# Making the slots' token numbers in two runs of small matmuls in the set-up of a mixture-of-experts kernel

## The reference, cut to what matters

```
gate = xn @ wg_W + wg_b + (genre_embed @ gg_W + gg_b)
gate_w = softmax(gate)
topk_w, topk_i = top_k(gate_w, 2)            # two of eight experts per token
h1 = relu(x @ W1[e] + b1[e]); h2 = relu(h1 @ W2[e] + b2[e])
out_e = h2 @ W3[e] + b3[e]
out = sum over e of out_e * cw[e]            # cw: weight of the chosen experts, else 0
```

## Time and profile before

| | |
|---|---|
| time, median of 3 runs | 742.73 us (741.77 to 743.66) |
| time of the profiled execution | 744.68 us |
| its span, first to last instruction | 743.2 us |
| mean granted TensorE clock over the span | 0.986 of full speed |
| PE busy | 713.3 us, 96% |
| DVE, ACT, POOL busy | 65%, 39%, 12% |

### The profile page before, as it was taken

The page is one execution under the profiler, slowest core; times in us unless marked ns, Lnnn a source line. Parts: engine busy times, 40 slices in busy tenths (PEclk is TensorE's granted clock), DMA queues, the critical chain, the costliest instruction groups (busy, mean ns, idle before and its releaser), DMA issues.

```text
span 743.2 us, 20463 instructions
## 1 busy us (share of the span) xinstructions
PE 713.3 (96%) x8266; PEld 615.5 (83%) x8266; DVE 486.3 (65%) x1036; ACT 287.8 (39%) x839; POOL 90.9 (12%) x102
## 2 busy tenths in 40 slices
PE   6389999999999999999999999999999999999997
PEld 4279999559999999978778878978888897888785
DVE  4756565743545444334777787787778778777867
ACT  3032121142121221253465446445544654564552
POOL 2121112411111101031101101110110111000000
PEclk9599999999999999999999999999999999999999
DMA  7998111217111102310001000000110010000000
GB/s 262 336 353 322 37 37 56 81 43 257 50 37 37 37 30 69 118 50 23 16 9 30 30 7 25 30 23 10 30 31 9 23 30 24 8 16 16 9 9 23
DMA packets 21402, 49.13 MB, mean 66 GB/s; under 512 B 3323, under 2 KB 14971, under 8 KB 18749
## 3 DMA queue, kind: packets, MB, share of 16 engines
q1 hardware_dynamic: 12256, 32.47, 12.2%
q0 software_dynamic: 3744, 10.49, 4.7%
q10 hardware_dynamic: 5309, 4.87, 2.0%
HBM read 41.00 MB, written 6.82 MB: 64 GB/s over the span
## 4 chain that ended last, share of the span: by engine, by line
PE 94%; DVE 3%; ACT 1%; issue 1%; another core or an unknown queue 0%; DVEq 0%; POOL 0%; ACTq 0%; POOLq 0%
PE ps L897 16%; PE ps L796 15%; PE ps L766 8%; PE ps L923 8%; PE ps L830 7%; PE ps L982 7%; PE ps L948 4%; PE ps L998 3%; PE ps L941 2%; PE ps L973 2%; PE ps L1013 2%; PE ps L1075 2%; PE ps L1032 2%; PE ps L790 1%; PE ps L676 1%; PE ps L1045 1%
## 5 line engine op out<-in xcount | busy, mean ns | idle before, releaser
L897 PE MATMUL ps<-arena,l_weights 128*128 128x128 f32 x1024 | 125.9, 277 | 0.5 <-ACT arena L1470 0.5
L796 PE MATMUL ps<-h_t,w_now 128*128 128x128 f32 x1056 | 123.4, 275 | 1.2 <-DVE h_t L1951 1.2
L796 PEld LDWEIGHTS ps<-h_t,w_now 128*128 128x128 f32 x1056 | 120.5, 192 | 1.4 <-issue 1.4
L897 PEld LDWEIGHTS ps<-arena,l_weights 128*128 128x128 f32 x1024 | 119.3, 192 | 2.3 <-ACT arena L1470 1.0
L1395 ACT ACTIVATE h_t<-ps,cols 128x128 f32<-128x128 f32 x132 | 37.8, 367 | 163.9 <-PE ps L766 149.5
L1926 DVE COPY w_now<-arena 128x2048 f32 x33 | 40.5, 1227 | 83.2 <-PE ps L796 74.7
L1476 ACT ACTIVATE arena<-ps,cols 128x128 f32<-128x128 f32 x256 | 73.9, 387 | 48.0 <-PE ps L897 48.0
L645 POOL DMA_INDIRECT arena<-expert_out,slot_of x32 | 33.1, 1033 | 323.0 <-DVE arena L1979 272.8
L766 PEld LDWEIGHTS ps<-xg_t,w_now 128*128 128x128 f32 x528 | 63.4, 192 | 6.0 <-ACT xg_t L1378 3.5
L766 PE MATMUL ps<-xg_t,w_now 128*128 128x128 f32 x528 | 65.0, 276 | 3.0 <-ACT xg_t L1378 3.0
L612 POOL DMA_INDIRECT xg<-in_x,slot_tok x36 | 41.6, 1155 | 186.4 <-PE ps L745 157.4
(11 more groups left out here) (366 smaller groups left out, 1097.1 us busy)
## 6 DMA issues: line engine op xcount, KB each, us to landing
arena<-in_experts SPq DMA_DIRECT2D x16, 1024.0 KB
expert_out<-y ACTq DMA_DIRECT2D x36, 128.0 KB
arena<-in_x_t SPq DMA_DIRECT2D x2, 1024.0 KB, 6.2
arena<-in_x SPq DMA_DIRECT2D x16, 128.0 KB
out<-arena SPq DMA_DIRECT2D x16, 128.0 KB, 1.7
b<-in_b SPq DMA_DIRECT2D x1, 1024.0 KB
l_weights<-in_wq SPq DMA_DIRECT2D x1, 1024.0 KB
l_weights<-in_wk SPq DMA_DIRECT2D x1, 1024.0 KB
```

The costliest lines, as they stand in the source:

```text
L796: last = mm(ps[:, 2, m * P:(m + 1) * P], w2_now[:, k, m * P:(m + 1) * P], h1_t[j % 2][:, k, :], start=k == 0, stop=k == KM - 1)
L897: last = mm(ps[:, b, c * P:(c + 1) * P], wt[:, k, f:f + P], m_t[:, k, :], start=k == 0, stop=k == KH - 1)
```

## The change

The token numbers of the first eight slot tiles are made first. `hi_hot` and `hi_ids` are made for tiles 0 to 7 only (128 x 256 elements each) before `lo_hot`, and PE's first run of 32 matmuls has 8 moving columns. The other 28 tiles (128 x 896 elements of each table) follow: their `hi_hot` is made after `starts_le` and ahead of the first copy to `slot_tok`, their `hi_ids` right after that copy, and it raises `hot_set` for the third time. PE makes their token numbers in a second run of 32 matmuls with 28 columns into bank 1, which stands among the constant matmuls: `keep_busy(40)` becomes `keep_busy(8)`, the second run, `keep_busy(8)`. DVE copies the second result just ahead of the last step of the gate weights, and POOL waits for it (`ids_set` at 2) ahead of the gather of tile 8.

```diff
@@ gpsimd, gathers @@
                 if j >= XG:
                     pool.wait_ge(xt_ps, j - XG + 1)
+                if j == EXP:
+                    pool.wait_ge(ids_set, 2)
                 pool.indirect_dma_start(
@@ tensor @@
                 for two in range(2):
-                    last = mm(bank(0, SLOT_TILES), lo_hot[:, m, :, two], hi_ids[:, m, :, two],
+                    last = mm(bank(0, EXP), lo_hot[:, m, :, two], hi_ids[:, m, 0:EXP, two],
                               start=m + two == 0, stop=m + two == N2)
             last.then_inc(ids_ps, 1)
...
-            keep_busy(40)
+            keep_busy(8)
+            pe.wait_ge(hot_set, 3)
+            for m in range(N2):
+                for two in range(2):
+                    last = mm(bank(1, SLOT_TILES - EXP), lo_hot[:, m, :, two], hi_ids[:, m, EXP:SLOT_TILES, two],
+                              start=m + two == 0, stop=m + two == N2)
+            last.then_inc(ids_ps, 1)
+            keep_busy(8)
@@ vector @@
-            step(tt(hi_hot, by_pair(hi_f, SLOT_TILES), table(iota_hi_h, SLOT_TILES), ALU.is_equal))
-            step(tt(hi_ids, hi_hot, by_pair(ids_h, SLOT_TILES), ALU.mult))
+            late = SLOT_TILES - EXP
+            step(tt(hi_hot[:, :, 0:EXP], by_pair(hi_f, EXP), table(iota_hi_h, SLOT_TILES)[:, :, 0:EXP], ALU.is_equal))
+            step(tt(hi_ids[:, :, 0:EXP], hi_hot[:, :, 0:EXP], by_pair(ids_h, EXP), ALU.mult))
...
                     bc(tile_start[0:1, 0:EXP], 3 * EXP), ALU.is_le))
+            step(tt(hi_hot[:, :, EXP:SLOT_TILES], by_pair(hi_f, late), table(iota_hi_h, SLOT_TILES)[:, :, EXP:SLOT_TILES], ALU.is_equal))
             dve.wait_ge(ids_ps, 1)
-            dve.tensor_copy(slot_tok[:, :], bank(0, SLOT_TILES)).then_inc(ids_set, 1)
+            dve.tensor_copy(slot_tok[:, 0:EXP], bank(0, EXP)).then_inc(ids_set, 1)
+            tt(hi_ids[:, :, EXP:SLOT_TILES], hi_hot[:, :, EXP:SLOT_TILES], by_pair(ids_h, late), ALU.mult).then_inc(hot_set, 1)
             step(red(segment_f[0:1, 0:EXP], starts_le[0:1, 0:EXP], X, ALU.add))
...
             step(red(gate_inv, eq, X, ALU.add))
+            dve.wait_ge(ids_ps, 2)
+            dve.tensor_copy(slot_tok[:, EXP:SLOT_TILES], bank(1, late)).then_inc(ids_set, 1)
             tt(weight_of[:, 1, :], gate_inv, weight_of[:, 0, :], ALU.mult).then_inc(arena_free, 1)
             dve.wait_ge(arena_free, 1)
```

## The result

The changed kernel takes 744.58 us, the median of 20 runs (741.98 to 748.75), beside 743.15 us for the kernel before (20 runs, 741.77 to 745.83): ratio 1.0025, 95% interval 1.0013 to 1.0036. That is slower, by 0.25%: less than the 0.3% that the prediction took as the least that counts, but outside its range of 741.0 to 744.2. The medians hide what happened. Each run comes with its mean granted clock, and that sorts these 20 without exception: 0.985 or 0.986 in the five, 0.984 to 0.978 in the fifteen.

What follows compares the result with a forecast made beforehand. PE's queue of work bounds the kernel, so only the first `layer1`'s start can move: 0.15 us from landing plus 0.1 at PE, said 0.3. From the median, 742.73 - 0.3 = 742.4 us; range 741.0 to 744.2.

Steps and rivals of the forecast that it cites:

- the late clock: Rival: the clock rises only after the first tile's `layer1`, 744.4 us, or the second's, 746.4; chance 0.12, a third beyond the first.
- the busy stretch up to 35.6: Argument against a late clock: PE's work up to 35.6 is as long as the stretch that brought the rise.
- the signs that it named for being wrong: First `layer1`: clock there at 0.50, start before 38.0, or the first expert's weights copied (L1910) after the first `xg_t`.
- Tables, first run, first copy, issue: Set-up on DVE, PE, POOL: 256-element tables 295 ns each, first copy about 31.25, first gather issued at 31.74, 0.81 us earlier.
- PE's queue: PE ahead of the first transposes: constant matmuls end at 35.5 to 35.7, free 1.2 us earlier; DVE waits about 1 us.
- The copy of the first expert's weights: L1910 on DVE: done at 37.1, its cover ahead of `layer1` shrinking from 1.8 us to about 1.3.
- That cap: The weights' copy keeps `layer1` from starting before 37.15, limiting the gain to 1.8 us, 740.9 us; chance 0.08.
- Landing: First gather's arrival: 0.15 us earlier, between 0 and 0.81, the experts' load perhaps holding it.
- The rival in which the landing follows the issue: Rival: the first gather lands a fixed time behind its issue; gain 0.8 us, 741.9 us, chance 0.20.
- The 1.2 us behind the transposes: Between the first transposes' end, 37.27, and ACT's copy, 38.50: carried as an unknown without a cause.
- The forecast without the clock: Start of the first `layer1`: 0.15 for landing plus 0.1 for PE's lateness, said 0.3 us earlier; chance 0.42.
- two rivals (0.8 and 1.8): Landing follows the issue: gain 0.8 us, chance 0.20; the 1.2 us vanish as well, capped gain 1.8 us, chance 0.08.

Runs made afterwards that it cites:

- e14: The changed kernel unaltered, profiled once more: 743.97 us at a mean clock of 0.983.
- e5: The changed kernel unaltered, profiled once more: 745.01 us at a mean clock of 0.983.
- e16: The changed kernel unaltered, profiled once more: 741.80 us at a mean clock of 0.985.
- e17: The changed kernel with the second run directly behind the f32 matmuls and all 16 constant matmuls behind it: 746.11 us, ratio 1.0038.
- e10: The kernel before with SP's 1024 KB load of the third biases moved behind the next expert's load: 743.27 us, ratio 1.0001.
- e2: The kernel before with 16 constant matmuls in place of 40: 743.91 us, ratio 1.0010.
- e4: The changed kernel with the second run directly behind the f32 matmuls and 36 constant matmuls behind it: 742.49 us, ratio 0.9994.
- e8: The kernel before with 80 constant matmuls added behind the ranks' matmuls, ahead of the slots': 743.67 us, ratio 1.0015.
- e1: The changed kernel with 28 constant matmuls in place of the last 8: 743.27 us, ratio 1.0005.
- e13: The kernel before with its 40 constant matmuls replaced by 8 of 128 columns, 32 of 28 and 8 of 128: 742.67 us, ratio 1.0002.
- e3: The kernel before with 26 constant matmuls in place of 40: 742.93 us, ratio 1.0008.
- e9: The changed kernel with SP's 1024 KB load of the third biases moved behind the next expert's load: 743.92 us, ratio 1.0006.
- e11: The changed kernel with the second run directly behind the f32 matmuls, 24 constant matmuls behind it, third biases loaded behind the next expert: 742.10 us, ratio 0.9987.
- e12: e4's kernel timed again: 743.15 us, ratio 0.9999.
- e7: The changed kernel with 80 constant matmuls added ahead of the slots' matmuls and 40 in place of the last 8: 743.61 us, ratio 1.0009.

## Why the prediction was wrong

The step that failed is the one on the clock. The prediction held the late clock for a rival with a chance of 0.12, since "the busy stretch up to 35.6 is as long as the one that brought the rise", and it put at nothing that a clock which has risen can fall again behind a pause. A low clock was the case in 15 of 20 runs, and in two of the seven profiled executions of the changed kernel: the first `layer1` took 3.46 us after no rise (e14) and 3.33 after a fall (e5), in place of 2.05. Of the signs that it named for being wrong, all three came: the clock at 0.50 in the first `layer1` (e14), that `layer1` before 38.0 (37.38 in the profile after), and the copy of the weights ending behind the first `xg_t` (e14, e16).

- **Tables, first run, first copy, issue.** Right: 0.29 us each, copy at 31.24 (31.25 said), issue at 31.70 (31.74).
- **PE's queue.** Right: free at 35.46 (35.5 to 35.7 said), the second result a wait of 1.0 us for DVE.
- **The copy of the first expert's weights.** Right as a term, 36.84 where the bound was to end at 37.1. The cover was summed wrongly (1.8 us shrinking to 1.3: by its own figures the copy ended at 36.13 before, which is 2.8 ahead of 38.93, and 37.1 is 1.5 ahead of 38.63), and in five of seven profiles there was none: where the gather landed early, `layer1` waited 0.8 to 1.1 us for the weights, 0.3 to 0.6 more than for ACT. That cap was the right one, and it is not what made the kernel slower (e17).
- **Landing.** Taken as 0.15 us earlier; 0.4 in the profile, and 3.0 to 6.0 us behind the issue over seven. It was argued as one number from one execution. That a load holds it was right, as e10 and e5 show. The 0.4 is mostly the load's own: its last packet goes at 35.97 in the profile before and at 35.63 after, which the change does not touch. The rival in which the landing follows the issue holds only where no load stands in the way (e10).
- **The 1.2 us behind the transposes.** They are in no later profile: in the profile after, ACT starts 0.09 us behind them. They belonged to that one execution, as did the wait at 133.66; its span of 743.2 beside 740.1 to 741.0 in the profiles of after that kept their clock says little of the change. Their cause stays open.
- **The forecast without the clock.** 0.3 us was said; the five runs that kept the clock give 743.1 - 742.1 = 1.0, between two rivals (0.8 and 1.8), and the shorter queue alone gives as much: e2, with filler taken out and nothing else, has 741.75 in such runs. These runs are picked by their clock, and a late landing costs clock as well as time (e5), so that part of the 1.0 may be the picking. Nor does an earlier start carry through whole: from the end of the first `layer1` on, the profiles of the changed order take 701.1 us (e4 701.5), those of the old one 700.8 to 701.0 without the two single waits of 1.2 and 1.1 us (before, e8); no run tells why.
- **The clock.** That argument from the busy stretch was true and not to the point. The place of the rise moves from execution to execution. In six of the seven profiles of the changed kernel it came 0.1 to 1.1 us behind the last constant matmul, and in e14 4.5 us behind it, in e17 7.6, with the first `layer1` run wholly or nearly so at 1.2 GHz; and where it has come, a pause takes it back (e5, e2). In the profile of before the constant matmuls ran 1.4 us past the rise and up to the gather's landing; they produced nothing, and were still the cover that counted. The prices named for the late clock, 744.4 and 746.4, are near the two heaps of runs (744.1 to 745.2 and 745.8 to 748.8), but in part by luck: the first tile was priced at 2.0 us on a start of 742.4. What the clock cost in a profile is 1.3 to 1.7 us, the first `layer1` at 3.33 to 3.78 in place of 2.05, on 742.05; in e5 and e17 the rest of the loss is the late landing.

Settled is that PE's earlier end brings the fault (e1, e2, e17), that the later copy is not needed for it (e17; e2, where it stands as before), and that 28 columns alone do not bring it (e13). Open is why its share rises so steeply: 5 of 24 runs where PE ends 3.93 to 3.99 us behind the gather's issue (e3, e13), 15 of 20 and 11 of 12 at 3.76; and why it is no higher, 7 of 12, where PE ends earliest (e2, 3.08). In e3 and e13 gather and PE's end both come later against the load of `b3`, which the change does not move, so the gather waits less for it (it lands 2.9 and 3.2 us behind its issue); e9 agrees in part. No run was made that moves this alone. Nor was an execution at 0.979 (746 to 749 us) caught in a profile. If a lower mean is time at half speed, (0.985 - 0.979) x 742 / 0.5 = 9 us more at 1.2 GHz would cost up to 4.5 us, an estimate that brings 742.05 to 746.5, the low end of these runs; where the 9 us lie, and what the rest is, was not seen.

## What to carry to other kernels

Work that produces nothing may be what keeps the clock: before shortening it, see in the windows of several executions when the granted clock rises, whether the filler runs past that in all of them, and whether anything (a gather, a copy of weights) can still make the engine pause before the real work flows. Sort the executions by mean clock; the one profile of this change came from the fastest quarter of a kernel that is slower in the median. Where useful matmuls take the filler's place, put them first and the filler last, to end just behind the latest arrival; here that, with the load that held the arrival moved away (e11), made the change a gain of 0.13%, measured once, while without that move it gained nothing (e4, e12).

## What was not expected of the hardware

The granted clock falls back within the first tile when PE has paused 1.9 to 2.4 us just after the rise (e2, e5), and also while DVE makes the tables after an early rise (e7, e8). A gather of 128 rows behind a 1024 KB load lands 2.9 to 6.0 us after its issue, and 3.0 to 3.2 with that load moved; it lands 0.4 to 0.9 us behind the load's last packet, which can go up to 1.9 us after the load's other closing packets (e5). In the profile of before ACT saw the end of two transposes 1.2 us late, and in none of 19 later profiles was it so again.
